# A lead of 28 first-layer slots instead of 30, a small memset behind each indirect transfer, and one staging tile less, in a routed feed-forward kernel

## The reference

```python
z1 = einsum('bfi,bir->bfr', x, v[:, 0]) / 512            # r = 16
z  = einsum('bfr,bor->bfo', z1, u[:, 0]) / 16
g  = gelu(einsum('bfi,oi->bfo', x, W) + fc_bias + z + cond, approximate=False)
prob = softmax(g @ w_router + b_router)                  # 16 experts
mask = one_hot_any(top_k(prob, 4))
h = relu(einsum('nd,ebd->neb', g, w1b) + b1b)            # 16 blocks of 128
y = einsum('neb,ebd,ne->nd', h, w2b, mask) + b2
out = x + y
```

## Time and profile before

| what | value |
|---|---|
| the profiled execution's own time | 1100.98 us |
| its span | 1099.1 us |
| TensorE matmul | 850.5 us busy, 77% of the span |
| VectorE | 825.7 us, 75% |
| ScalarE | 578.6 us, 53% |
| GpSimd | 576.5 us, 52% |
| mean granted TensorE clock | 0.898 |
| DMA, mean over the span | 323 GB/s |
| median of the 3 runs | 1100.98 us |

### The profile page before, as it was taken

One profiled execution on the slowest core, in us unless ns is written; L12 is line 12 of the kernel. 1 busy time (PEld: TensorE's weight loads), 2 busy tenths in 40 slices (PEclk: granted clock), 3 DMA queues, 4 the chain that ended last, 5 costly groups with the idle time before them and its releaser, 6 DMA issues.

```text
span 1099.1 us, 18009 instructions
## 1 busy us (share of the span) xinstructions
PE 850.5 (77%) x4924; PEld 677.5 (62%) x4924; DVE 825.7 (75%) x1964; ACT 578.6 (53%) x1061; POOL 576.5 (52%) x591
## 2 busy tenths in 40 slices
PE   8999998999999999999998989999999900000000
PEld 6777776778777777777776667888888700000000
DVE  4565557777676777768678987789998679888787
ACT  5565565766676676667666776767676600000000
POOL 1377777676666666666667777555555620000000
PEclk9999999999999999999999999999999955555555
DMA  6699789999898998989789999799876689999999
GB/s 185 221 364 344 264 288 371 305 326 309 292 330 298 307 311 309 314 304 324 269 295 341 325 326 319 280 337 335 296 273 230 221 351 418 425 433 429 427 429 387
DMA packets 103234, 354.82 MB, mean 323 GB/s; under 512 B 29961, under 2 KB 29961, under 8 KB 92384
## 3 DMA queue, kind: packets, MB, share of 16 engines
q1 hardware_dynamic: 59104, 217.21, 56.9%
q0 software_dynamic: 43936, 136.37, 31.5%
q10 hardware_dynamic: 96, 0.10, 0.0%
HBM read 200.47 MB, written 169.65 MB: 337 GB/s over the span
## 4 chain that ended last, share of the span: by engine, by line
PE 60%; DMA 15%; DVE 7%; ACT 7%; issue 6%; POOL 3%; ACTq 2%; POOLq 0%; SPq 0%; DVEq 0%
PE lay L1097 13%; PE hid L1205 12%; PE yps L1236 12%; DMA w2l<-yt 11%; PE trn L1190 7%; PE hid L1210 6%; PE trn L1118 3%; PE hid L1083 3%; DVE stx L960 2%; POOL xg L495 2%; ACT gsb L601 2%; DMA outT<-ys 2%; PE lay L1236 2%; PE rps L1133 1%; ACTq L612 1%
## 5 line engine op out<-in xcount | busy, mean ns | idle before, releaser
L521 POOL DMA_INDIRECT yt<-ys,ids x218 | 229.1, 1051 | 137.3 <-ACT ys L660 79.9
L495 POOL DMA_INDIRECT xg<-grow,ix x224 | 223.2, 996 | 108.5 <-issue 64.3
L769 DVE TENSOR_TENSOR gsb<-trn,gsb 128x512 fp32r<-128x512 f32 x239 | 161.1, 687 | 116.9 <-ACT gsb L601 116.1
L1097 PE MATMUL lay<-w2l,xs 128*128 128x512 f32 x768 | 191.0, 398 | 0.0
L1097 PEld LDWEIGHTS lay<-w2l,xs 128*128 128x128 f32 x768 | 142.4, 190 | 29.8
L601 ACT ACTIVATE gsb<-trn 128x512 fp32r<-128x512 f32 x239 | 142.6, 597 | 14.1 <-PE trn L1190 13.5
L1190 PE MATMUL trn<-idf,gr 128*128 128x128 f32 x956 | 144.8, 274 | 4.5 <-DVE gsb L769 4.2
L1190 PEld LDWEIGHTS trn<-idf,gr 128*128 128x128 f32 x956 | 115.1, 140 | 40.5 <-DVE gsb L769 14.7
L1205 PE MATMUL hid<-gsb,w1c 128*128 128x512 f32 (+1 forms) x576 | 127.9, 364 | 0.0
L1236 PE MATMUL yps<-w2c,hh 128*128 128x512 f32 x336 | 119.9, 438 | 6.9 <-issue 5.8
L629 ACT ACTIVATE hv<-hid,b1c 128x512 f32<-128x512 f32 (+1 forms) x94 | 52.7, 584 | 134.6 <-PE hid L1210 133.7
(11 more groups left out here) (206 smaller groups left out, 1647.3 us busy)
## 6 DMA issues: line engine op xcount, KB each, us to landing
gr<-xg SPq DMA_DIRECT2D x49, 1056.0 KB
xs<-yt SPq DMA_DIRECT2D x16, 2048.0 KB, 19.5
w2l<-yt SPq DMA_DIRECT2D x15, 2048.0 KB, 19.6
gr<-xg SPq DMA_DIRECT2D x45, 528.0 KB
stx<-xT SPq DMA_DIRECT2D x64, 256.0 KB, 3.9
outT<-ys SPq DMA_DIRECT2D x31, 512.0 KB, 20.4
xg<-xrow SPq DMA_DIRECT2D x16, 528.0 KB, 6.5
w2f<-xrow SPq DMA_DIRECT2D x16, 512.0 KB, 13.4
```

What stands on the lines that cost most here:

```text
L495: pool.indirect_dma_start(out=xg, out_offset=bass.IndirectOffsetOnAxis(ap=ix[:, row_buffer(b), q, k:k + 1], axis=0), in_=grows[row_buffer( ...
L521: pool.indirect_dma_start(out=yt, out_offset=bass.IndirectOffsetOnAxis(ap=ids[:, j % 8, c:c + 1], axis=0), in_=yss[result_buffer(j)][:, c, ...
L769: dve.tensor_tensor(gsb[:, :, LO, c * P:(c + 1) * P], turned[TURN_BANK[n]][:, :].rearrange("p (k t) -> p k t", k=KC), gsb[:, :, HI, c * P: ...
L1097: pe.matmul(lay[s % 2][:, :], xs[:, b % 2, k, h, cols], wls[:, k, a, :], start=(k == 0 and a == HI and h == HI), stop=False)
```

## The change

LAG goes from 30 to 28. So each tile's steps stand two slots earlier, the program has 100 slots, and the slots with both layers are 36. SyncE loads each tile j in slot LAG + j - 2, the first two included: tile 0 in slot 26 as before, tile 1 in slot 27. GpSimd gets a function `rest`, which follows each of the row and result transfers: a memset of a tile `pace` of 128 x 16, which waits for the memset before it. There are 256 transfers of rows and 286 of results, so 542 memsets. The tile `hval` goes; `half_rows` writes into `tval` and waits first until the last transfer from `tval` is done.

```diff
-LAG = 30
+LAG = 28
...
-        hval = sb("hval", [NE, 2, 4], I32)
...
+        pace = sb("pace", [P, 16], F32)
...
-                if j in (-4, -2):
-                    load_tile(j // 2 + 2)
-                if 2 <= j + 2 < NTILE:
+                if 0 <= j + 2 < NTILE:
                     load_tile(j + 2)
...
-            for values in (tval, hval):
-                pool.iota(values[:, :, 0], [[0, 2]], base=0, channel_multiplier=1).then_inc(g_k, 1)
-                pool.memset(values[:, :, 1:4], 0).then_inc(g_k, 1)
+            pool.iota(tval[:, :, 0], [[0, 2]], base=0, channel_multiplier=1).then_inc(g_k, 1)
+            pool.memset(tval[:, :, 1:4], 0).then_inc(g_k, 1)
...
+            paced = [0]
+
+            def rest():
+
+                if paced[0] > 0:
+                    pool.wait_ge(g_pace, paced[0])
+                pool.memset(pace[:, :], 0.0).then_inc(g_pace, 1)
+                paced[0] += 1
+
             def place_rows(b, q):
...
                         in_=grows[row_buffer(b)][:, q, :], in_offset=None).then_inc(s_sc[row_buffer(b)][q], 16)
+                    rest()
...
-                                            in_=hval[:, h, :], in_offset=None).then_inc(s_tb, 16)
+                                            in_=tval[:, h, :], in_offset=None).then_inc(s_tb, 16)
...
                     oob_is_err=False).then_inc(s_y[result_buffer(j)], 16)
+                rest()
...
                 if n == 0:
-                    dve.wait_ge(g_k, 11)
-                elif n < NB:
+                    dve.wait_ge(g_k, 9)
+                else:
                     dve.wait_ge(s_tb, 16 * n)
...
-                step(dve.tensor_copy(hval[:, 0, 2:3], tskip[:, :]))
+                step(dve.tensor_copy(tval[:, 0, 2:3], tskip[:, :]))
```

More of the change, by code:

```diff
@@ L278, in adaln_ffn @@
         s_gr = [sem(f"s_gr_{n}") for n in range(2)]
-        g_z, g_id, g_up, g_tok, g_k, g_s = (
-            sem(n) for n in ("g_z", "g_id", "g_up", "g_tok", "g_k", "g_s"))
+        g_z, g_id, g_up, g_tok, g_k, g_s, g_pace = (
+            sem(n) for n in ("g_z", "g_id", "g_up", "g_tok", "g_k", "g_s", "g_pace"))
         p_z, p_w, p_r, p_lt, p_rk, p_cnt, p_pos, p_tn, p_f1, p_y = (
@@ L894, in half_rows @@
                 step(dve.scalar_tensor_tensor(tskip[:, :], tnum[:, :], float(HALF), cnt[:, :], ALU.mult, ALU.subtract))
-                step(dve.tensor_copy(hval[:, 0, 2:3], tskip[:, :]))
+                step(dve.tensor_copy(tval[:, 0, 2:3], tskip[:, :]))
                 step(dve.tensor_tensor(tskip[:, :], tover[:, :], tskip[:, :], ALU.subtract))
                 step(dve.tensor_tensor(tover[:, :], tover[:, :], cnt[:, :], ALU.add))
[L898 to L901, removed]
+                step(dve.tensor_copy(tval[:, 0, 1:2], tskip[:, :]))
+                step(dve.tensor_scalar(tval[:, 0, 3:4], tskip[:, :], float(HALF - 1), None, ALU.add))
+                step(dve.tensor_scalar(tval[:, 1, 1:2], tover[:, :], -float(HALF), None, ALU.add))
+                dve.tensor_scalar(tval[:, 1, 3:4], tover[:, :], -1.0, None, ALU.add).then_inc(v_tb, 1)
             def split_w1(j, h):
```

## The result

The changed kernel takes 1114.13 us, the median of 4 runs (1112.36 to 1116.27); the kernel before took 1102.24 beside it (1099.98 to 1104.48). The ratio is 1.0105, 95% interval 1.0081 to 1.0130. It is slower, as forecast, and the time lies in the range (1105 to 1160), but the change costs 11.9 us and not the 25 that 1126 stands for. Its profiled execution took 1113.2 us.

A forecast was written before the change was run, and what follows sets the result against it. TensorE bounds the slots with both layers, DMA the final sum; TensorE's waits decide. 1100.98 + 8.0 (tile 1) + 8.0 (memsets) + 7.1 (tile 45) + 4.8 (memsets) - 3.1 (slots) = 1125.8, so 1126 us; range 1105 to 1160.

The forecast's parts named there:

- The memsets, 8.0 + 4.8 us: GpSimd behind: 0.10 us per memset, delaying batch 4's last rows by 8.0 us and those before tile 45 by 4.8.
- two memsets in a row (0.05): Alternative reading by GpSimd's spacing of starts at the beginning: memset terms of 4.0 and 2.4 us, sum 1119.4.
- The wait at tiles 0 and 1, 8.0 us: TensorE reaches tile 1's turns at 155.9, tile 1 arrives at 163.94: 8.0 us wait; tile 0 perhaps late within it.
- Tile 45 in slot 72, 7.1 us: Tile 45, turned in slot 72 instead of 74, arrives at 650.7; TensorE is there at 643.58 and waits 7.1 us.
- The table's wait, 4.3 us under cover of tile 45: VectorE waits 4.3 us for slot 69's table transfer before half_rows; inside tile 45's 7.1 us, so not added.
- The exchange of two slots, -3.1 us: Two first-layer slots (4.91 each) and two experts-alone slots (8.72) go, two of both (12.07) come: -3.1 us.
- Rival B: Memset costs over 0.15 us, GpSimd bounds the slots with both layers: 1164, or 1231 at 0.40 us; chance 0.13.
- C: Memset fills the gap between GpSimd's transfers, which come closer together, step below 1.26 us: 1095 us; chance 0.06.
- D: Only the first wait comes: memset free, tile 45 and the table land in time: 1106 us; chance 0.09.

The follow-up runs named there:

- the two traces named above: The changed kernel without its 542 memsets, 1111.55 us; and the kernel before with only LAG at 28 and its loads, without memsets and with hval, 1113.78 us.

## Why the prediction was wrong

The direction and the place of the loss were right; a price was wrong. By its own steps:

- **The memsets, 8.0 + 4.8 us: the step that failed.** They cost nothing: the step of GpSimd is 1.27 us with and 1.26 without, the kernel with the memsets alone is at 1.0009 [0.9997, 1.0022], and the changed kernel without them is at 1.0085 with an interval that overlaps its own. The error was in taking the duration of a row (0.10, in truth 0.14) for its cost. The earlier trace rows showed 0.30 us behind each transfer in which the engine issued nothing; the prediction named this as the lower bound, 0, and went by the row that was nearest in shape. Without the term its sum is 1113.0, and 1114.13 was measured. The Trainium skill, Perfetto Trace Analysis, section GPSIMD Engine Instruction, says to time GpSimd by the spacing of starts; the runs agree with it, and by transfer-to-transfer spacing the price is 0.01. The prediction had applied it to two memsets in a row (0.05), which still left 6.4 us too much.
- **The wait at tiles 0 and 1, 8.0 us: right.** It was 7.1 us in this trace, and 8.8 to 9.5 in those of the four other kernels with this lead and at most one memset. It began at tile 0 and not, as the main line had it, at tile 1; the prediction said that this would only bring forward a part of the same wait, and the ratios with tile 0 loaded early or late say so for `LAG = 29` (1.0051 and 1.0046).
- **Tile 45 in slot 72, 7.1 us: right in kind, 4.4 in size.** From issue to load (3.4) and load to turn (7.2) were as taken. But TensorE came to slot 72's turns at 668.90 - 3.50 = 665.4, 21.8 us later than before, and GpSimd to the last rows only 18.5 later, so 3.3 of the 7.1 were gone; by the stretch as a whole the wait is worth 4.4 (3.0 to 5.3 in the two traces named above).
- **The table's wait, 4.3 us under cover of tile 45: right.** Alone it costs 4.5 us, in the changed kernel nothing: the lead alone, without it, is no faster (1113.78).
- **The exchange of two slots, -3.1 us: -0.1.** Two slots of both kinds are indeed 24.1 us (tile 1 to 33 is 560.50 - 174.40 = 386.1 for 32). But the two that vanish are worth (24.1 - 9.76) / 2 = 7.2 each and not 8.72: 14 slots of experts alone took 121.62, 8.69 each, and the 12 that are left take 131.38 - 24.1 = 107.3, 8.94 each. Half of this stood in the trace of before. The two slots that no longer lie in the stretch are 76 and 77, and they took 686.17 - 670.40 = 15.8 us there, 7.9 each: the prediction read its 8.72 from slots 74 and 75. That is 1.7 of the 3.0 us missed. The other 1.4 are that slots 64 to 75 take 107.3 us with the changed lead and took 670.40 - 564.55 = 105.9 before; why was not tried.
- **Rival B** is refuted for one memset and shown for four (1442 us). At 0.40 us a memset its terms add up to 1232 and not 1231. **C** had the memset filling the gap right, but the transfers don't come closer together. **D**, 1106, had the memset free, and missed that tile 45 is late.

The terms as measured in the one trace: 7.1 + 0 + 4.4 + 0 - 0.1 = 11.4 us, against 11.9 between the medians. That they meet so closely is in part luck, since either wait differs by 2 us from trace to trace. In the profiled executions the difference is 12.2: 11.4, less the 1.35 of the start, and 2.1 that fall on one tile,

```profile
807.25 0.84 ACT L637 ACTIVATE hv<-hid,b1c 128x256 f32<-128x256 f32 x2 [2.26 <-PE hid L1218]
817.21 0.84 ACT L637 ACTIVATE hv<-hid,b1c 128x256 f32<-128x256 f32 x2 [2.28 <-PE hid L1218]
```

9.96 us from tile 61 to 62 where 7.85 is usual. At this tile it is 7.9 in three other kernels with memsets and 8.8 in the one with the memsets alone, so I take it for chance.

What stays open: why the engine is idle for 0.30 us behind a transfer, and why a second memset costs 0.14 in some steps and 0.43 in others; and what each of the two waits of `LAG = 32` is worth. On chips that run the kernel before at 1101 us no version tried beats it.

## What to carry to other kernels

Price an added instruction by what it does to the spacing of its engine's starts, not by its duration: look for idle time that is already in each step and that the newcomer can fill. Where an engine has a backlog, what its step grows by counts once for each step ahead of the deadline, so the size of the step deserves the most care; here 0.24 us more on 79 steps, 18.6 us, came out as 18.3 in the kernel's time. And a lead is bounded from both sides: too short and the first tiles are late, too long and the producer meets its buffers.

## What the runs showed that I had not expected

A 128x16 memset of 0.13 us between two indirect transfers of GpSimd adds 0.01 us to the step; the second adds 0.24 in the mean, and four make the step 1.75 us. One slot less of lead cost 5 us and two cost 12, while two more cost 22.5. And one chip ran the same kernel before at 1292 us instead of 1101, and the changed kernel without memsets, with GpSimd waiting 82.6 us for VectorE, was 1.0% faster there.
